# The maxima's score products take the step after: one offset in an attention kernel's interleaving

## The chip, the cores and the metric

The kernel runs on one core of one Trainium2 chip. The metric is the device time of one execution in microseconds (us), the median of several. The kernel before takes 2329.86 us (three runs, 2328.88 to 2336.1).

## The reference

The reference is a small network of several layers: an attention block with a feed-forward part, a routed layer of experts, a selective scan and a second gated layer. The change touches the attention alone. For two sequences of 2048 tokens and sixteen heads (eight of each of two attentions) of width 8 it computes:

```
q = (xin @ wq.T + bq).reshape(b, s, H, DK)
k = (xin @ wk.T + bk).reshape(b, s, H, DK)
v = (xin @ wv.T + bv).reshape(b, s, H, DK)
scores = jnp.einsum('bshd,bthd->bhst', q, k) * (1.0 / np.sqrt(DK))
a = jax.nn.softmax(scores, axis=-1)
o = jnp.einsum('bhst,bthd->bshd', a, v).reshape(b, s, DH)
```

## The kernel before, in words

The attention is cut into 32 units, one head of one sequence each. A unit's scores are computed twice. First the maximum of each row is needed: TensorE multiplies queries by keys, and VectorE reduces the product. This is done in 32 chunks a unit, each 128 queries by 1024 keys: two matmuls of 512 columns (L1593, the rows 0 to 47 and 64 to 111 of the tile `stacks`), into two banks of PSUM, and one reduction over 1024 values (L805). There are two such pairs of banks, so chunk c can be written only when the reduction of chunk c - 2 is done; that is the wait at the head of `max_scores`. When all 32 chunks are reduced, VectorE runs five small operations (L807 to L813) before it reduces the next unit's chunk 0. TensorE transposes their result (L1599), ScalarE copies it to `mT` (L1229), and SyncE's queue copies that twice into `stacks` (L518), from where the unit's exponentials take it as three more rows of the product.

Then the scores are computed again in 64 blocks of 128 keys by 512 queries (L1639), ScalarE takes the exponential into `probs` (L1241), and TensorE weighs the values with it (L1611). The blocks go in 44 steps a unit: one block in the even steps, in step 37 and in step 43, two blocks in the other odd steps. Steps take turns in two PSUM buffers, so the product of step e waits for the exponential of step e - 2. A weighing covers four blocks: eight matmuls in the trace, in two rounds of four, placed where its four exponentials lie at least two steps back: 16 a unit, at steps 1, 4, 7, 9, 12, 15, 17, 20, 23, 25, 28, 31, 33, 36, 39, 42. A half unit's sums stand in one bank, which ScalarE copies out (L1225) after the exponentials of steps 1 and 23, once the weighing of that step is done.

The order on TensorE is written out by hand. Each step issues, in this order: its one or two score products; the transpose, in step 37; one chunk of maxima, if the count by that step allows one; one weighing, if one is due. The maxima run ahead of the exponentials by a unit and ten chunks (`AHEAD`), so a unit's last chunk (31) and the next one's first (0) fall in the last third of a unit's steps. There are 32 chunks to 44 steps, so 12 steps have none. VectorE and ScalarE only follow: their order has no gaps to choose.

In this text a step's E is its score product, M the chunk of maxima, W the weighing.

Of the kernel before, what the change touches and what calls it, by code (L numbers as in the profile page):

```python
# [21 lines left out]
UNITS = G * B  # L22
# [10 lines left out]
STEPS = 2 * TCH  # L33
DFF = 512
CHUNKS = 2 * TCH
EXPS, TURN, AHEAD = 44, 37, 10
E, NG, KTOP, GTOP = 32, 8, 4, 4
CAP = int(1.25 * N * KTOP / E)
LN4, LN9 = NB, 5 * NB
# [73 lines left out]
def after(eng, sem, count):  # L113

    if not isinstance(count, int) or count > 0:
        eng.wait_ge(sem, count)
# [23 lines left out]
def build(nc, a, out):  # L140
# [3 lines left out]
    with ExitStack() as ctx:  # L144
# [1374 lines left out]
        def _(pe):  # L1519
# [77 lines left out]
            def turn_max(uu):  # L1597
                pe.wait_ge(spl_ready, uu + 1)
                pe.transpose(PT[:, 0:P], spl.rearrange("p l c -> p (l c)"), identb[:, :]).then_inc(mt_ready, 1)  # L1599

            def weigh(u, pair, w):

                pe.wait_ge(exp_done, EXPS * u + EXP_OF[4 * pair + 3] + 1)
                if pair % (TCH // 2) == 0:
                    after(pe, o_evac, 2 * u + pair // (TCH // 2))
                for odd in range(2):
                    kt = (2 * pair + odd) % TCH
                    for qb in range(2):
                        jg = 2 * odd + qb
                        at = (6 * (w % 2) + 4 * pair + jg) % RING * 512  # L1610
                        mm = pe.matmul(OB[32 * jg:32 * jg + 32, :], VH[w][:, kt, :], probs[:, at:at + 512],  # L1611
                                       start=(kt < 2), stop=(kt >= TCH - 2))
                mm.then_inc(pv_done, 1)

            def max_chunk(m):
                u, n = divmod(m, CHUNKS)
                if n == 0:
                    pe.wait_ge(qk_ld[u % 4], 192 * (u // 4 + 1))
                max_scores(u, n, u % 4)
# [8 lines left out]
            weighed, chunk = 0, CHUNKS + AHEAD  # L1628
            for u in range(UNITS):
                w, final = u % 4, u == UNITS - 1  # L1630
                pe.wait_ge(m_ld[w], 32 * (u // 4 + 1))
                for e, (first, blocks) in enumerate(EXP):
                    after(pe, exp_done, EXPS * u + e - 1)
                    if e == TURN + 2 and not final:
                        pe.wait_ge(mt_out, u + 2)
                    for i in range(blocks):
                        o = 64 * i
                        kt, q0 = (first + i) // 2 % TCH, (first + i) // 2 // TCH * 1024 + (first + i) % 2 * 512
                        mm = pe.matmul(EXB[e % 2][:, i, :], KS[w][o:o + KROWS + 3, kt * P:(kt + 1) * P], QS[w][o:o + KROWS + 3, q0:q0 + 512],  # L1639
                                       start=True, stop=True)  # L1640
                    mm.then_inc(sc_ready, 1)
                    if e == TURN and not final:
                        turn_max(u + 1)
                    if chunk < min(CHUNKS * UNITS, CHUNKS * (u + 1) + AHEAD + CHUNKS * (e + 1) // EXPS):
                        max_chunk(chunk)
                        chunk += 1
                    if e == 1:
                        pe.wait_ge(vh_ready, u + 1)
                    wu, pair = divmod(weighed, TCH)
                    if EXPS * wu + EXP_OF[4 * pair + 3] <= EXPS * u + e - 2:  # L1650
                        weigh(wu, pair, wu % 4)
                        weighed += 1
# [391 lines left out]
```

## Time and profile before

| | |
|---|---|
| median of three runs | 2329.86 us |
| the profiled execution | 2333.52 us |
| its span, first to last instruction | 2331.7 us |
| TensorE matmuls, busy | 1911.9 us, 82% |
| VectorE, busy | 1838.0 us, 79% |
| ScalarE, busy | 1425.0 us, 61% |

The span starts at the first instruction. The attention's steps lie between some 295 and 1640 us of it. Shares are of the whole span, so a stage has to be read from its own window.

### The profile page before, as it was taken

The page shows a single profiled execution, that of the slowest core. Times are in us where ns is not written, and L with a number is a line of the kernel's source. Part 1 is how long each engine was busy: PE and PEld are TensorE (multiplying, and loading weights), DVE is VectorE, ACT ScalarE, POOL GpSimd, SP SyncE. Part 2 cuts the span into 40 slices and gives each one's busy share as a digit, 9 for nine tenths or more (in the row PEclk, how much of TensorE's full clock was granted, in tenths as well). Part 3 has the DMA queues.
Part 4 walks back from the last instruction along what each step waited for, and adds up shares of the span by engine and source line. Part 5 has one row for each costly group of instructions (what it writes and reads, how often), then busy time and mean ns, then how long its engine had stood idle before and what let it go on. Part 6 is the DMA issues. An engine that isn't in the chain of part 4 may idle for free.

```text
span 2331.7 us, 33796 instructions
## 1 busy us (share of the span) xinstructions
PE 1911.9 (82%) x11886; PEld 727.7 (31%) x11886; DVE 1838.0 (79%) x2868; ACT 1425.0 (61%) x2159; POOL 298.3 (13%) x371
## 2 busy tenths in 40 slices
PE   2768488888888888888888888888898788679895
PEld 1324011221222112222222222221676444346563
DVE  3774789999999999999999999992334888658778
ACT  1113078787887878878878788778432334457542
POOL 0000100000000000422222222200003765000000
PEclk9976589999999999999999999999999878879896
DMA  4023101111111110211111111101575443222231
GB/s 123 19 74 122 54 22 52 32 51 39 34 55 33 40 50 31 73 39 36 45 33 45 37 34 45 47 9 30 161 205 157 119 128 87 77 83 58 74 94 37
DMA packets 156247, 150.76 MB, mean 65 GB/s; under 512 B 34490, under 2 KB 131774, under 8 KB 156094
## 3 DMA queue, kind: packets, MB, share of 16 engines
q1 hardware_dynamic: 147742, 131.48, 19.2%
q0 software_dynamic: 8352, 17.29, 2.6%
q8 instruction: 90, 1.47, 0.3%
q14 instruction: 63, 0.52, 0.1%
HBM read 85.81 MB, written 62.13 MB: 63 GB/s over the span
## 4 chain that ended last, share of the span: by engine, by line
PE 64%; DVE 14%; ACT 13%; issue 3%; DMA 2%; SPq 2%; POOL 0%; ACTq 0%; DVEq 0%; POOLq 0%
PE PS L1611 22%; PE PS L1639 14%; ACT probs L1241 10%; PE PS L1593 7%; DVE mxp L805 5%; PE PS L1686 3%; PE PS L1742 1%; PE PS L1842 1%; PE PS L1860 1%; PE PS L1673 1%; PE PS L1751 1%; ACT SG L1225 1%; PE PS L1863 1%; DMA xs_d<-SG 1%; PE PS L1845 1%
## 5 line engine op out<-in xcount | busy, mean ns | idle before, releaser
L805 DVE TENSOR_REDUCE mxp<-PS 128x1 f32<-128x1024 f32 x1024 | 1203.3, 1220 | 131.9 <-PE PS L1593 126.7
L1241 ACT ACTIVATE probs<-PS 128x512 f32<-128x512 f32 (+1 forms) x1408 | 1041.4, 790 | 261.9 <-PE PS L1639 259.4
L1639 PE MATMUL PS<-stacks 51*128 51x512 bf16 x2048 | 539.9, 385 | 139.3 <-ACT probs L1241 135.7
L1593 PE MATMUL PS<-stacks 48*128 48x512 bf16 x2048 | 513.6, 391 | 74.7 <-DVE mxp L805 51.2
L1611 PE MATMUL PS<-probs,VH 128*32 128x512 f32 x4096 | 547.3, 606 | 2.6 <-ACT probs L1241 0.7
L1639 PEld LDWEIGHTS PS<-stacks 51*128 51x128 bf16 x2048 | 136.0, 93 | 799.4 <-ACT probs L1241 761.5
L1510 POOL DMA_INDIRECT VP<-oe_d,ROWI x128 | 132.8, 1037 | 329.1 <-DMA oe_d<-stacks 266.5
L1492 POOL DMA_INDIRECT xe_d<-xn_s,rows_s x128 | 124.5, 973 | 382.9 <-PE PS L1611 353.6
L1593 PEld LDWEIGHTS PS<-stacks 48*128 48x128 bf16 x2048 | 121.5, 95 | 142.8 <-DVE mxp L805 96.1
L1611 PEld LDWEIGHTS PS<-probs,VH 128*32 128x32 f32 x4096 | 81.6, 108 | 191.4 <-issue 152.2
L826 DVE TENSOR_TENSOR stacks<-stacks,PS 128x640 f32<-128x640 f32 x32 | 26.2, 819 | 130.6 <-ACT stacks L1273 130.6
L1482 POOL COPY VH<-VP 128x128 f32<-128x128 f32 (+1 forms) x32 | 9.2, 293 | 744.6 <-PE PS L1611 599.4
L1686 PE MATMUL PS<-stacks,ews 128*128 128x320 f32 x256 | 76.4, 441 | 6.1 <-DVE stacks L826 4.3
L1742 PE MATMUL PS<-wa,wff 128*128 128x512 f32 x64 | 42.5, 821 | 25.7 <-ACT wa L1296 25.7
L1273 ACT ACTIVATE stacks<-PS 128x640 f32<-128x640 f32 x32 | 22.5, 704 | 59.9 <-PE PS L1686 59.9
L1686 PEld LDWEIGHTS PS<-stacks,ews 128*128 128x128 f32 x256 | 46.0, 189 | 27.5 <-issue 9.0
L1229 ACT ACTIVATE mT<-PS 48x128 bf16<-48x128 bf16 x32 | 8.2, 257 | 63.9 <-PE PS L1599 63.9
L1225 ACT ACTIVATE SG<-PS 128x512 f32<-128x512 f32 x64 | 38.2, 597 | 12.5 <-PE PS L1611 12.5
L1527 PE MATMUL PS<-ident,wa 128*128 128x128 f32 x32 | 8.9, 434 | 42.9 <-DVE wa L136 42.9
L1673 PEld LDWEIGHTS PS<-ews,stacks 128*128 128x128 f32 x320 | 40.7, 192 | 6.5 <-DVE stacks L826 1.6
L1673 PE MATMUL PS<-ews,stacks 128*128 128x128 f32 x320 | 41.0, 275 | 1.4 <-DVE stacks L832 1.4
L1842 PE MATMUL PS<-VP,cst 128*128 128x512 f32 x64 | 35.2, 677 | 7.0 <-DVE VP L1000 7.0
(351 smaller groups left out, 1997.9 us busy)
## 6 DMA issues: line engine op xcount, KB each, us to landing
xe_d<-zt SPq DMA_DIRECT2D x16, 640.0 KB
stacks<-xe_d SPq DMA_DIRECT2D x32, 320.0 KB, 3.6
oe_d<-stacks SPq DMA_DIRECT2D x32, 320.0 KB, 2.8
o_d<-SG SPq DMA_DIRECT2D x256, 32.0 KB, 1.6
ews<-in_ew_dram SPq DMA_DIRECT2D x33, 192.0 KB, 2.3
stacks<-ql_d SPq DMA_DIRECT2D x64, 96.0 KB
stacks<-kl_d SPq DMA_DIRECT2D x64, 96.0 KB
probs<-xs_d SPq DMA_DIRECT2D x18, 256.0 KB, 3.6
```

The source lines that it names most:

```text
L805: v.tensor_reduce(mxp[:, n // 2, n % 2:n % 2 + 1], MXB[n % 2].rearrange("p a c -> p (a c)"), X_AX, ALU.max).then_inc(mx_done, 1)
L1225: act.activation(OE[half][:, :], OB, ACT.Copy).then_inc(o_evac, 1)
L1241: act.activation(probs[:, at:at + n * 512], EXB[e % 2][:, 0:n, :].rearrange("p a c -> p (a c)"), ACT.Exp, scale=float(1.0 / np.sqrt(np.flo ...
L1492: pool.indirect_dma_start(xe_d, bass.IndirectOffsetOnAxis(rows_s[i][:, n:n + 1], 0), xn_s[i][:, :], None, bounds_check=E * CAP - 1, oob_is ...
L1510: pool.indirect_dma_start(GB[:, t % (2 * TB), n, :], None, oe_d, bass.IndirectOffsetOnAxis(ROWI[:, t, n:n + 1], 0), bounds_check=E * CAP, ...
L1593: mm = pe.matmul(MXB[n % 2][:, i, :], QS[w][o:o + MAXROWS, (n // 2) * P:(n // 2 + 1) * P], KS[w][o:o + MAXROWS, key:key + 512], start=True ...
L1611: mm = pe.matmul(OB[32 * jg:32 * jg + 32, :], VH[w][:, kt, :], probs[:, at:at + 512], start=(kt < 2), stop=(kt >= TCH - 2))
L1639: mm = pe.matmul(EXB[e % 2][:, i, :], KS[w][o:o + KROWS + 3, kt * P:(kt + 1) * P], QS[w][o:o + KROWS + 3, q0:q0 + 512], start=True, stop=True)
L1673: mm = pe.matmul(o, hhe[w % 2][:, t * P:(t + 1) * P], EW[w][:, 2, :], start=True, stop=True)
L1686: mm = pe.matmul(PS[:, 2 + 2 * m + h, 0:CAP // 2], EW[w][:, m, :], xeT[w % 2][:, h * CAP // 2:(h + 1) * CAP // 2], start=True, stop=True)
L1742: pe.matmul(PS[:, 2 + f % 2, :], wff1[:, f * P:(f + 1) * P], f_(wa[3]), start=True, stop=True).then_inc(f_ready, 1)
L1842: pe.matmul(PS[:, b, :], BELOW, scaled[:, b, :], start=True, stop=True)
```

## The change

In the count that allows a chunk of maxima, 12 is added before the division by 44 steps (`EARLY`).

```
-EXPS, TURN, AHEAD = 44, 37, 10
+EXPS, TURN, AHEAD, EARLY = 44, 37, 10, 12
...
-                    if chunk < min(CHUNKS * UNITS, CHUNKS * (u + 1) + AHEAD + CHUNKS * (e + 1) // EXPS):
+                    if chunk < min(CHUNKS * UNITS, CHUNKS * (u + 1) + AHEAD + (CHUNKS * (e + 1) + EARLY) // EXPS):
                         max_chunk(chunk)
                         chunk += 1
```

32 times 44 steps plus 12 still gives 32 chunks a unit. The steps without a chunk were 0, 3, 7, 11, 14, 18, 22, 25, 29, 33, 36, 40; they are now 1, 4, 8, 12, 15, 19, 23, 26, 30, 34, 37, 41. So the pattern stands one step later, with one chunk more already done at each of its places. Nothing changes on any engine but TensorE, and there no instruction of the attention is added or taken away.

TensorE in steps 10 to 15 of a unit (L1639 is E, L1593 is M, L1611 is W; neighbours of one line are joined). Before:

```order
L1639 MATMUL PS<-stacks 128x512
L1593 MATMUL PS<-stacks 128x512 x2
L1639 MATMUL PS<-stacks 128x512 x3
L1593 MATMUL PS<-stacks 128x512 x2
L1611 MATMUL PS<-probs,VH 32x512 x4
L1639 MATMUL PS<-stacks 128x512 x2
L1593 MATMUL PS<-stacks 128x512 x2
L1639 MATMUL PS<-stacks 128x512 x3
L1593 MATMUL PS<-stacks 128x512 x2
L1611 MATMUL PS<-probs,VH 32x512 x4
```

The same steps of TensorE now:

```order
L1639 MATMUL PS<-stacks 128x512
L1593 MATMUL PS<-stacks 128x512 x2
L1639 MATMUL PS<-stacks 128x512 x2
L1593 MATMUL PS<-stacks 128x512 x2
L1639 MATMUL PS<-stacks 128x512
L1611 MATMUL PS<-probs,VH 32x512 x4
L1639 MATMUL PS<-stacks 128x512 x2
L1593 MATMUL PS<-stacks 128x512 x2
L1639 MATMUL PS<-stacks 128x512
L1593 MATMUL PS<-stacks 128x512 x2
L1639 MATMUL PS<-stacks 128x512 x2
L1611 MATMUL PS<-probs,VH 32x512 x4
```

The chunks that stood between E and W in steps 12 and 15 now follow E of steps 11 and 14, which have no W.

TensorE in steps 29 to 33, around the chunks 31 and 0 of two units, before:

```order
L1639 MATMUL PS<-stacks 128x512 x3
L1593 MATMUL PS<-stacks 128x512 x2
L1639 MATMUL PS<-stacks 128x512 x2
L1593 MATMUL PS<-stacks 128x512 x2
L1611 MATMUL PS<-probs,VH 32x512 x4
L1639 MATMUL PS<-stacks 128x512
L1593 MATMUL PS<-stacks 128x512 x2
L1639 MATMUL PS<-stacks 128x512 x2
L1611 MATMUL PS<-probs,VH 32x512 x4
```

The same steps now:

```order
L1639 MATMUL PS<-stacks 128x512 x2
L1593 MATMUL PS<-stacks 128x512 x2
L1639 MATMUL PS<-stacks 128x512 x3
L1593 MATMUL PS<-stacks 128x512 x2
L1611 MATMUL PS<-probs,VH 32x512 x4
L1639 MATMUL PS<-stacks 128x512
L1593 MATMUL PS<-stacks 128x512 x2
L1639 MATMUL PS<-stacks 128x512 x2
L1593 MATMUL PS<-stacks 128x512 x2
L1611 MATMUL PS<-probs,VH 32x512 x4
```

Chunk 31 moved from step 30 to 29. Steps 31, 32 and 33 now have one chunk each, the last of them between E and W of step 33, where there was none.

TensorE in steps 37 to 39 (L1599 is the transpose), before:

```order
L1639 MATMUL PS<-stacks 128x512
L1599 MATMUL PS<-identb,spl 128x128
L1593 MATMUL PS<-stacks 128x512 x2
L1639 MATMUL PS<-stacks 128x512
L1593 MATMUL PS<-stacks 128x512 x2
L1639 MATMUL PS<-stacks 128x512 x2
L1593 MATMUL PS<-stacks 128x512 x2
L1611 MATMUL PS<-probs,VH 32x512 x4
```

The same steps now:

```order
L1639 MATMUL PS<-stacks 128x512
L1599 MATMUL PS<-identb,spl 128x128
L1639 MATMUL PS<-stacks 128x512
L1593 MATMUL PS<-stacks 128x512 x2
L1639 MATMUL PS<-stacks 128x512 x2
L1593 MATMUL PS<-stacks 128x512 x2
L1611 MATMUL PS<-probs,VH 32x512 x4
```

The chunk of step 37 went to step 36; steps 38 and 39 keep theirs, so there are two in a row ahead of this W and not three. Steps 26 to 28 changed in the same way.

## Rows read from the trace of the kernel before

**Rows 1.** The page's first part: busy us, share of the span, instructions.

```profile
PE 1911.9 (82%) x11886; PEld 727.7 (31%) x11886; DVE 1838.0 (79%) x2868; ACT 1425.0 (61%) x2159; POOL 298.3 (13%) x371
```

**Rows 2.** Busy time in the attention's steady stretch: PE, PEld, DVE, ACT, POOL, clock, DMA.

```profile
340.00:1592.00 1252.00, 1094.43 (x7642) 252.63 (x7641) 1143.16 (x1101) 1002.13 (x1398) 145.10 (x220) 1.00 0.13 41
```

**Rows 3.** The copies of a half unit's sums: duration ns, first and last start.

```profile
L1225 ACT ACTIVATE SG<-PS x57: 597/597/597, 405.0 to 1584.0; 128x512 f32<-128x512 f32 x57
```

**Rows 4.** Groups by line, 396 to 1592 us: busy us, mean ns | idle before.

```profile
L805 DVE TENSOR_REDUCE mxp<-PS 128x1 f32<-128x1024 f32 x908 | 1068.6, 1220 | 99.1 <-PE PS L1593 94.2
L1241 ACT ACTIVATE probs<-PS 128x1024 f32<-128x1024 f32 x569 | 581.9, 1023 | 94.2 <-PE PS L1639 92.4 <-issue 0.4
L1639 PE MATMUL PS<-stacks 51*128 51x512 bf16 x1819 | 479.3, 383 | 122.2 <-ACT probs L1241 119.7
L1593 PE MATMUL PS<-stacks 48*128 48x512 bf16 x1816 | 449.5, 380 | 27.2 <-DVE mxp L805 27.2
L1241 ACT ACTIVATE probs<-PS 128x512 f32<-128x512 f32 x681 | 403.5, 597 | 134.4 <-PE PS L1639 134.0
```

**Rows 5.** Chain that ended last, steps 1 to 15: start us, us, what.

```profile
803.82 0.22 PE PS L1593 x2
...
806.63 0.22 PE PS L1593 x2
806.85 0.99 PE PS L1611 x8
...
810.99 0.22 PE PS L1593 x2
...
814.04 0.22 PE PS L1593 x2
...
817.14 0.22 PE PS L1593 x2
```

**Rows 6.** Timeline of ScalarE: steps 1 and 23, the copies of sums.

```profile
805.10 0.60 ACT L1225 ACTIVATE SG<-PS 128x512 f32<-128x512 f32 x1 [0.16 <-PE PS L1611]
...
826.11 0.60 ACT L1225 ACTIVATE SG<-PS 128x512 f32<-128x512 f32 x1 [0.22 <-PE PS L1611]
```

**Rows 7.** Timeline of TensorE, steps 26 to 29: start us, us, what [idle before <-releaser].

```profile
827.85 0.39 PE L1639 MATMUL PS<-stacks 51*128 51x512 bf16 x1
...
828.92 0.39 PE L1639 MATMUL PS<-stacks 51*128 51x512 bf16 x1
829.78 0.39 PE L1593 MATMUL PS<-stacks 48*128 48x512 bf16 x2 [0.47 <-DVE mxp L805]
...
831.10 0.39 PE L1639 MATMUL PS<-stacks 51*128 51x512 bf16 x2
```

**Rows 8.** Timeline of VectorE around the end of a unit's maxima.

```profile
828.50 4.69 DVE L805 TENSOR_REDUCE mxp<-PS 128x1 f32<-128x1024 f32 x4 [0.65 <-PE PS L1593]
...
834.16 1.22 DVE L805 TENSOR_REDUCE mxp<-PS 128x1 f32<-128x1024 f32 x1
```

**Rows 9.** Timeline of steps 37 to 39: the transfer of `mT`, E and M.

```profile
839.62 1.62 SPq L518 DMA_DIRECT2D stacks<-mT  x2
...
839.66 0.39 PE L1639 MATMUL PS<-stacks 51*128 51x512 bf16 x2
840.54 0.39 PE L1593 MATMUL PS<-stacks 48*128 48x512 bf16 x2 [0.49 <-DVE mxp L805]
```

**Rows 10.** Timeline of TensorE: E of steps 31 and 32.

```profile
832.67 0.39 PE L1639 MATMUL PS<-stacks 51*128 51x512 bf16 x2 [0.75 <-ACT probs L1241]
...
834.20 0.39 PE L1639 MATMUL PS<-stacks 51*128 51x512 bf16 x1
```

**Rows 11.** DMA traffic of 836 to 848 us in 40 slices, GB/s.

```profile
GB/s 0 0 0 0 0 0 0 0 0 0 0 0 0 0 0 0 3 38 0 20 76 0 0 0 0 0 0 0 0 0 0 0 0 0 0 0 0 0 0 0
```

**Rows 12.** Timeline of TensorE: the next unit's first E.

```profile
844.91 0.38 PE L1639 MATMUL PS<-stacks 51*128 51x512 bf16 x1
```

## The prediction

> **What bounds the kernel now.** I first read the page's busy shares [rows 1]: TensorE leads, but over a whole span of different layers. So the second view is the window of the attention's steady stretch [rows 2]. There VectorE is busy 1143 of 1252 us (91%), TensorE 1094 (87%), ScalarE 1002 (80%), and TensorE's clock is granted in full (1.00, the 2.4 GHz level). No engine is full. The pace comes from the copies of half a unit's sums [rows 3]: 57 of them are 56 half units, so a unit takes (1584.0 - 405.0) / 28 = 42.1 us. The stretch of the next view, 1196 us, is 28.4 units.
>
> Third, the groups with the idle time before them [rows 4]. All three engines wait for one another: VectorE's reductions wait 99.1 us for TensorE, 3.5 us a unit; the exponentials wait 94.2 + 134.4 = 229 us for TensorE; TensorE waits 122 us for exponentials and 27.2 us for VectorE, the last being 0.96 us a unit. A ring of dependencies sets the pace, so what counts is what stands between one exponential and the next product. Fourth, the chain that ended last. It goes through every W, and an M is on it only where W follows at once, or where TensorE runs behind anyhow: in steps 1, 4, 8, 12 and 15 each shows as a piece of 0.22 us [rows 5], the two matmuls of a chunk side by side. Where an M is not on the chain (steps 2, 5, 6, 13 and others) TensorE is waiting for an exponential and the M fills the wait. So an M costs 0.22 us in two kinds of places and nothing elsewhere: in a W step, and in the step between two W that are two steps apart (8, 16, 24, 32). Fifth, the timeline where M itself waits. In step 28 E starts at 828.92 and M at 829.78, 0.86 us later where 0.22 is the rule: 0.64 us lost [rows 7]. In step 39 it is 840.54 - 839.66 - 0.22 = 0.66 us [rows 9]. Together 1.30 us a unit, more than the 0.96 that the groups book to the matmuls, since part is booked to the weight loads. Both times W stands behind the waiting M, and behind W the next E, and so ScalarE. Both are the third of three steps in a row with a chunk (26, 27, 28 and 37, 38, 39): two buffers, and a third chunk that must wait for the first one's reduction.
>
> **The change, part by part.** No instruction of the attention comes or goes, so there is no cost of work, only of place. Per unit:
>
> *Slots taken off the path.* Steps 4, 12 and 15 keep W and lose M, and step 8, between two W, loses its M: 4 x 0.22 = 0.88 us. Steps 1 and 23 lose theirs too, but behind their W ScalarE's copy waits, and it can start earlier only until it meets the exponential before it: it waited 0.16 and 0.22 us [rows 6], so 0.38 is gained. Sum 1.26. The M's go to steps 0, 3, 11, 14, 22, which have no W and lie beside exponentials; there TensorE's wait for the exponential hides them. Without that cover each would cost 0.22 again.
>
> *Slots put on the path.* Steps 7, 25, 33 and 36 have W, had no M and get one: 4 x 0.22 = 0.88. Net of both, 0.38 us less.
>
> *Waits that go.* The row of three 26, 27, 28 becomes 27, 28, 29, and 37, 38, 39 becomes 38, 39, 40: in steps 28 and 39 M is now the second, with a buffer free, and the third has no W behind it. That takes off the 1.30 us.
>
> *Waits that come.* Rows of three whose third step has W are now 5, 6, 7 and 31, 32, 33. From one E to its reduction is 828.50 - 827.85 = 0.65 us [rows 7, 8], a reduction takes 1.22, and the next M follows 829.78 - 829.72 = 0.06 after it. So M of step 7 can't start before 0.65 + 1.22 + 0.06 = 1.93 us after E of step 5. By itself it would come at 1.57 + 0.22 = 1.79: with a double exponential between them, E of a step follows E of two steps before by 832.67 - 831.10 = 1.57 [rows 7, 10]. Wait: 0.14. In step 33 the two units' boundary lies between. Four reductions from 828.50 take 4.69, so they are (4.69 - 1.22) / 3 = 1.16 apart and the fourth starts at 831.97; the next unit's first starts at 834.16, 2.19 later, for the five small operations [rows 8]. Counting from E of step 29, now with chunk 31: reduction 0.65, that of chunk 0 not before 2.84, done 4.06, M of step 33 from 4.12. TensorE would get there by 1.57 (to E of 31) + 1.53 (its E, M and W; 834.20 - 832.67 [rows 10]) + 0.44 (E and M of 32) + 0.22 (E of 33) = 3.76. Wait: 0.36. Together 0.50. Bounds: nothing, if the steps ahead run later than I count, and 1.30, the two waits of before. I take 0.5, since it comes from the rows of just these instructions. Before, step 33 had no chunk, and just that gap gave VectorE time.
>
> Sum per unit: -0.38 - 1.30 + 0.50 = -1.18 us. Units 0 to 30 see all of it, 31 x 1.18 = 36.6. The last unit has no maxima after step 30, so it keeps -1.26 and the 0.64 of step 28, and pays steps 7 (0.22 + 0.14) and 25 (0.22): -1.3. Together -38 us.
>
> *What else hangs on the place.* The transfer of the next unit's maxima begins after step 37 at 839.62 [rows 9] and its last traffic lies in the slice of 842.0 to 842.3 [rows 11]; the next unit's first E, which needs it, is at 844.91 [rows 12]. The steps between shrink by some 0.6 us, so over 1.5 us of slack stay. VectorE's idle 3.5 us a unit falls to some 2.4, still not full.
>
> The sum is made against the profiled execution: 2333.5 - 38 = 2295.5 us. That execution lies 3.7 us above the median of the runs shown, so the median should be 2329.9 - 38 = 2292 us.
>
> **The rivals.** *Only slots.* The waits move but don't shrink: new ones of 1.3 us for old ones of 1.3 us. For it: chunks and buffers are the same, and so is the share of work. Against it: the count of the third step above. Per unit -0.38; 31 x 0.38 is 12 us, and 0.8 of the last unit (1.26 less 0.44) makes it 13: 2317.
>
> *No new waits.* Steps 7 and 33 come late enough for their buffers. For it: 0.14 and 0.36 us are small beside sums of four or five rows. Per unit -1.68, or 54 us in all with the last unit: 2276.
>
> *VectorE is the bound.* It has the highest share [rows 2], its work is unchanged, and what an earlier M gains is given back as a later wait of TensorE for it: no change, 2330. Against it: of its 3.5 us of idle a unit nearly all is waiting for TensorE [rows 4]. The Trainium skill, in "Perfetto Trace Analysis", section "Identifying the Most-Contended Engine", says to take the engine with the highest occupancy as the bottleneck and work on that first, which would name VectorE here and expect nothing from TensorE's order alone; the trace agrees on the occupancy (91%) but shows the remaining idle time to be made by that order.
>
> *Slower: VectorE falls behind at the units' boundary.* The old waits don't go, since a backlog built up by three chunks right behind the five small operations is still there in steps 38 and 39, and steps 7 and 33 wait as long as 28 and 39 did. Per unit -0.38 + 1.30 = +0.92, 28 us in all: 2358. It decides from the point where the waits of a unit come to more than 1.68 us. Against it: steps 34 and 37 have no chunk, and after step 33 the next M's needed reduction ends ahead of it by my count.
>
> **How the numbers follow.** Forecast 0.64, only slots 0.15, no new waits 0.09, VectorE the bound 0.06, slower by the boundary 0.06. 0.3%, 7 us, is about what a measurement of this kernel can tell from no change. Faster by more: the first three less 0.02 for slots that come to less, 0.86; within: 0.08; slower: 0.06. The forecast's own range is 2282 to 2304 (a wait of 0.2 to 0.9 a unit in place of 0.5). The range for 8 in 10 takes in the two faster rivals, 2275 to 2320, and leaves out no change and slower.
>
> **What would show it.** In the profile after, the copies of sums should stand 40.9 us apart per unit (every second one). TensorE's waits for VectorE should be gone in steps 28 and 39 and be found in step 33 (0.36 us between the slots) and, short, in step 7. VectorE's idle before its reductions should fall by about a third. The chain that ended last should carry no M in steps 1, 4, 12, 15 and 23, and one in 7, 25, 33 and 36. The forecast is wrong if waits of 0.6 us or more stand in steps 7 or 33, if the interval is not shorter by 0.7 us or more, or if the time after the attention changes.

## The result, and the profile after

The changed kernel takes 2289.34 us (median of six runs, 2279.61 to 2293.11), the kernel before 2328.49 us in the runs beside it (2323.88 to 2336.1). The ratio is 0.9825, 95% interval 0.980 to 0.985: 39 us or 1.7% faster. The forecast was 2292 us.

The profiled execution spans 2289.1 us. The steady stretch of the attention, in the columns of [rows 2]:

```profile
340.00:1550.00 1210.00, 1094.22 (x7627) 251.76 (x7623) 1131.06 (x1098) 994.28 (x1394) 144.71 (x219) 1.00 0.13 42
```

The copies of half a unit's sums, against [rows 3]:

```profile
L1225 ACT ACTIVATE SG<-PS x57: 597/597/598, 399.2 to 1542.0; 128x512 f32<-128x512 f32 x57
```

A unit takes (1542.0 - 399.2) / 28 = 40.81 us, where it took 42.11: 1.29 us less. Read from each unit's first exponential to the next one's, the first unit is 1.95 us shorter, the next 29 are 1.29 each, the one after them 1.44, and the last unit not at all (37.39 us to its last exponential's end in both traces): 40.9 of the 42.6 us by which the two spans differ. The other 1.7 us lie ahead of the first exponential (at 295.5 us before, 293.8 now), where the change does nothing. The clock is granted in full in this stretch as before. The rest of the kernel didn't change: after the last exponential 692.5 us remain, as they did before.

The groups of the stretch 396 to 1550 us (28.3 units), against [rows 4]:

```profile
L805 DVE TENSOR_REDUCE mxp<-PS 128x1 f32<-128x1024 f32 x904 | 1055.8, 1219 | 69.5 <-PE PS L1593 67.0
L1241 ACT ACTIVATE probs<-PS 128x1024 f32<-128x1024 f32 x566 | 578.9, 1023 | 65.9 <-PE PS L1639 61.6 <-issue 0.2
L1639 PE MATMUL PS<-stacks 51*128 51x512 bf16 x1812 | 476.6, 384 | 104.2 <-ACT probs L1241 95.7 <-ACT mT L1229 6.5
L1593 PE MATMUL PS<-stacks 48*128 48x512 bf16 x1806 | 443.4, 381 | 6.4 <-DVE mxp L805 5.5
L1241 ACT ACTIVATE probs<-PS 128x512 f32<-128x512 f32 x678 | 401.3, 596 | 140.0 <-PE PS L1639 139.9
```

No operation is faster. The idle time before the reductions fell from 3.5 to 2.5 us a unit, the wait of the maxima's matmuls for VectorE from 0.96 to 0.19 (5.5 / 28.3).

In steps 28 and 39 M stood 0.86 and 0.88 us behind E [rows 7, 9]. The timeline of TensorE after (start us, us, what [idle before <-releaser]); the first two rows are E and W of step 28, the others those of step 39:

```profile
810.27 0.39 PE L1639 MATMUL PS<-stacks 51*128 51x512 bf16 x1 [0.25 <-ACT probs L1241]
...
810.80 1.07 PE L1611 MATMUL PS<-probs,VH 128*32 128x512 f32 x8
...
821.17 0.39 PE L1639 MATMUL PS<-stacks 51*128 51x512 bf16 x2 [0.23 <-ACT mT L1229]
...
821.71 1.06 PE L1611 MATMUL PS<-probs,VH 128*32 128x512 f32 x8
```

From E to W is now 0.53 and 0.54 us; the waits are gone. New ones stand in steps 7 and 33 (E, M, W of each):

```profile
790.99 0.39 PE L1639 MATMUL PS<-stacks 51*128 51x512 bf16 x2 [0.47 <-ACT probs L1241]
791.42 0.39 PE L1593 MATMUL PS<-stacks 48*128 48x512 bf16 x2
791.74 1.06 PE L1611 MATMUL PS<-probs,VH 128*32 128x512 f32 x8
...
815.14 0.59 PE L1639 MATMUL PS<-stacks 51*128 51x512 bf16 x2
815.92 0.39 PE L1593 MATMUL PS<-stacks 48*128 48x512 bf16 x2 [0.19 <-DVE mxp L805]
816.24 1.07 PE L1611 MATMUL PS<-probs,VH 128*32 128x512 f32 x8
```

Both M are released by VectorE; in step 7 it is the row of M's weight load that shows it:

```profile
791.41 0.10 PEld L1593 LDWEIGHTS PS<-stacks 48*128 48x128 bf16 x2 [0.33 <-DVE mxp L805]
```

A difference of the starts of E and M (0.78 us in step 33) over-reads the second wait. My reading is that a matmul queued behind another is recorded some 0.2 us before it runs: E of step 33, which follows M of step 32 at once, has 0.59 us on record for 0.39. So E to W (0.75 and 1.10 us) is the safer measure. What it is without a wait is shown below.

The copies of sums in ScalarE's timeline, the first with the exponentials ahead of it, against [rows 6]:

```profile
784.93 2.17 ACT L1241 ACTIVATE probs<-PS 128x512 f32<-128x512 f32 x3 [0.59 <-PE PS L1639]
787.03 0.60 ACT L1225 ACTIVATE SG<-PS 128x512 f32<-128x512 f32 x1
...
807.36 0.60 ACT L1225 ACTIVATE SG<-PS 128x512 f32<-128x512 f32 x1
```

They wait for nothing now; each starts as the exponential before it ends.

The chain that ended last, steps 24 to 33 (start us, us, what):

```profile
807.88 5.81 DVE mxp L805 x5
...
813.71 0.20 DVE nmx L807
...
814.73 1.14 DVE mxp L805
815.88 0.05 issue
815.92 0.39 PE PS L1593 x2
816.31 0.99 PE PS L1611 x8
```

Here is what I had not foreseen. From 807.88 to 815.88 the chain stays on VectorE: five reductions, the five small operations, one more reduction, without a gap, for a fifth of each unit; on the chain from 396 to 1550 us L805 went from 5.9% to 16.9%. These shares don't say what VectorE costs there. With a reduction of half the length (below) steps 24 to 32 keep their times to 0.01 us and only step 33 falls, by 0.37. Over this stretch VectorE's row and the ring of the other two engines are nearly equally long, and VectorE's is longer by 0.37 us.

Since every unit repeats to 0.01 us, a step can be read by itself: the median time from the start of its exponential to the next, over units 2 to 29, in us.

| step | before | after | |
|---|---|---|---|
| 1, 4, 12, 15, 23 | 1.67, 1.23, 1.25, 1.59, 1.73 | 1.45, 1.01, 1.03, 1.37, 1.51 | M gone from a W step: 0.22 each |
| 9 | 1.42 | 1.19 | M gone from step 8, between two W |
| 28, 39 | 1.89, 2.19 | 1.28, 1.53 | the wait gone |
| 7 | 1.37 | 1.79 | M and a wait |
| 33 | 1.20 | 1.78 | M and a wait |
| 25, 36 | 1.19, 0.97 | 1.29, 1.21 | M |

### The profile page after: what moved, and what is told of

The parts are those of the page before. It is cut to its first block, busy times and chain, and to the rows that moved or that the text cites. A ratio compares the mean times of both kernels' runs of the same rounds, so it can differ in the third digit from the quotient of the medians.

```text
span 2289.1 us, 33796 instructions
## 1 busy us (share of the span) xinstructions
PE 1912.8 (84%) x11886; PEld 728.1 (32%) x11886; DVE 1829.0 (80%) x2868; ACT 1420.3 (62%) x2159; POOL 298.6 (13%) x371
## 4 chain that ended last, share of the span: by engine, by line
PE 58%; DVE 21%; ACT 12%; issue 3%; DMA 2%; SPq 2%; POOL 0%; ACTq 0%; DVEq 0%; POOLq 0%
PE PS L1611 18%; PE PS L1639 13%; DVE mxp L805 11%; ACT probs L1241 8%; PE PS L1593 5%; PE PS L1686 3%; PE PS L1742 2%; PE PS L1842 1%; PE PS L1860 1%; PE PS L1673 1%; PE PS L1751 1%; ACT SG L1225 1%; PE PS L1863 1%; DMA xs_d<-SG 1%; PE PS L1845 1%
## 5 line engine op out<-in xcount | busy, mean ns | idle before, releaser
L805 DVE TENSOR_REDUCE mxp<-PS 128x1 f32<-128x1024 f32 x1024 | 1194.4, 1218 | 99.5 <-PE PS L1593 96.8
L1639 PE MATMUL PS<-stacks 51*128 51x512 bf16 x2048 | 538.7, 385 | 121.0 <-ACT probs L1241 110.8
L1593 PE MATMUL PS<-stacks 48*128 48x512 bf16 x2048 | 508.7, 392 | 52.5 <-DVE mxp L805 28.1
L1611 PE MATMUL PS<-probs,VH 128*32 128x512 f32 x4096 | 546.5, 606 | 1.0 <-ACT probs L1241 0.7
L1639 PEld LDWEIGHTS PS<-stacks 51*128 51x128 bf16 x2048 | 135.9, 93 | 769.3 <-ACT probs L1241 723.0
L1593 PEld LDWEIGHTS PS<-stacks 48*128 48x128 bf16 x2048 | 116.5, 95 | 154.1 <-DVE mxp L805 106.8
L1611 PEld LDWEIGHTS PS<-probs,VH 128*32 128x32 f32 x4096 | 81.0, 108 | 169.6 <-issue 138.9
L1273 ACT ACTIVATE stacks<-PS 128x640 f32<-128x640 f32 x32 | 22.5, 704 | 59.6 <-PE PS L1686 59.6
L1264 ACT ACTIVATE stacks<-PS 128x640 f32<-128x640 f32 x32 | 22.5, 703 | 29.3 <-PE PS L1665 29.3
```

The costliest lines, as they stand in the source:

```text
L805: v.tensor_reduce(mxp[:, n // 2, n % 2:n % 2 + 1], MXB[n % 2].rearrange("p a c -> p (a c)"), X_AX, ALU.max).then_inc(mx_done, 1)
L1593: mm = pe.matmul(MXB[n % 2][:, i, :], QS[w][o:o + MAXROWS, (n // 2) * P:(n // 2 + 1) * P], KS[w][o:o + MAXROWS, key:key + 512], start=True ...
```

## The experiments

These ran on three other chips, here A, B and C, where the kernel before takes 2421.6, 2434.0 and 2420.1 us. The changed one ran again on C and takes 2384.0. Its unit is the same there to 0.01 us (40.82, below), so the time of a unit, read in each trace from the copies of sums ahead of 900 us, and the ratio to the kernel before on the same chip are what is compared. The kernel before was not profiled on A, B or C: its 42.11 us a unit are the first chip's. The times in the expectations were meant for the first chip; their differences stand. In the traces of A, B and C two or three units from the middle on are disturbed, and the layers after the attention take 770 to 791 us for 692.5. In the changed kernel on C it is 773.6, on nearly the same busy time (the last exponential's end to the last instruction; the first row is the changed kernel on C, the second on the first chip; after the two times PE, PEld, DVE, ACT, POOL, clock, DMA):

```profile
1606.40:2380.00 773.60, 583.62 (x3214) 382.29 (x3214) 472.42 (x1437) 303.39 (x565) 134.10 (x130) 0.85 0.34 96
```

```profile
1596.60:2289.10 692.50, 572.39 (x3214) 379.05 (x3214) 472.06 (x1437) 302.87 (x564) 135.79 (x130) 0.89 0.38 108
```

On C 11.7% of this stretch's chain, some 90 us, stand in waits whose releaser is "another core or an unknown queue"; the 200 longest pieces of the first chip's chain have none. What these waits are stays open; no comparison of units rests on them.

| kernel | chip | a unit, us | ratio to before [95%] |
|---|---|---|---|
| before | the first | 42.11 | |
| changed | C | 40.82 | 0.9864 [0.984, 0.989] |
| first half | A | 41.22 | 0.9894 [0.985, 0.994] |
| second half | A | 41.70 | 0.9962 [0.994, 0.999] |
| before, short reduction | A | 41.03 | 0.9803 [0.976, 0.985] |
| changed, short reduction | A | 40.25 | 0.9707 [0.967, 0.975] |
| AHEAD 11 | B | 42.11 | 1.0016 [1.000, 1.004] |
| EARLY 24 | B | 42.38 | 1.0044 [1.002, 1.007] |
| changed, gap at 33 | B | 40.87 | 0.9858 [0.982, 0.990] |
| changed, unit's end later | C | 40.59 | 0.9848 [0.982, 0.988] |
| gaps chosen, first | B and C | 40.03 | 0.9731 and 0.9763 |
| gaps chosen, second | C | 39.88 | 0.9745 [0.971, 0.978] |

**Half of the move each.** The steps without a chunk are listed and counted; only the list differs.

```
-EXPS, TURN, AHEAD = 44, 37, 10
+EXPS, TURN, AHEAD = 44, 37, 10
+WITHOUT = (1, 4, 8, 12, 15, 19, 23, 25, 29, 33, 36, 40)
...
-                    if chunk < min(CHUNKS * UNITS, CHUNKS * (u + 1) + AHEAD + CHUNKS * (e + 1) // EXPS):
+                    if chunk < min(CHUNKS * UNITS, CHUNKS * (u + 1) + AHEAD + sum(i not in WITHOUT for i in range(e + 1))):
```

> The first half of the move alone: the steps without a chunk are 1, 4, 8, 12, 15, 19, 23 as in the changed kernel, and 25, 29, 33, 36, 40 as before. Theory A (a chunk costs its 0.22 us where a weighing follows, and the wait for a buffer in some steps): steps 1, 4, 8, 12, 15, 23 give back 0.22 us each, 1.3 us, and step 7 costs 0.4; 0.9 us a unit less than before's 42.1, 28 us in all, about 2300 us. The waits in steps 28 and 39 stay as they were. Theory B (VectorE's pace alone decides, and only its waits in steps 28 and 39 were worth something): no change, 2328 us.

The second has `WITHOUT = (0, 3, 7, 11, 14, 18, 22, 26, 30, 34, 37, 41)`.

> The second half alone: the steps without a chunk are 0, 3, 7, 11, 14, 18, 22 as before, and 26, 30, 34, 37, 41 as in the changed kernel. Theory A: steps 28 and 39 give back 0.60 + 0.66 us, steps 25, 33 and 36 cost 0.09 + 0.58 + 0.24; 0.35 us a unit less, 11 us in all, about 2317 us, and with the first half it adds up to the whole. Theory B: the whole gain of 39 us, 2289 us.

The copies of sums (25 of them, 12 units) of the first half and of the second:

```profile
L1226 ACT ACTIVATE SG<-PS x25: 597/597/598, 382.0 to 876.6; 128x512 f32<-128x512 f32 x25
```

```profile
L1226 ACT ACTIVATE SG<-PS x25: 597/597/598, 377.6 to 878.1; 128x512 f32<-128x512 f32 x25
```

494.6 / 12 = 41.22 and 500.5 / 12 = 41.71 us: 0.89 and 0.40 us less than before, 0.9 and 0.35 expected. They add up to 1.29, the whole. Theory B falls: more than two thirds of the gain came without touching the waits of steps 28 and 39.

**A reduction of half the values.** VectorE reduces the first 512 of a chunk's 1024 values and leaves the other half out.

```
-v.tensor_reduce(mxp[:, n // 2, n % 2:n % 2 + 1], MXB[n % 2].rearrange("p a c -> p (a c)"), X_AX, ALU.max)
+v.tensor_reduce(mxp[:, n // 2, n % 2:n % 2 + 1], MXB[n % 2][:, 0, :], X_AX, ALU.max)
```

> The kernel before with every reduction of a chunk over 512 of its 1024 values only (the maximum is then that of half the keys); all matmuls stay, and VectorE takes about half the time. Theory A: only the waits in steps 28 and 39 go, 1.26 us a unit, 39 us: 2289 us. Theory B (VectorE is the bound): far more, VectorE's whole lead over the others, some 3 us a unit or 90 us: 2240 us.

> The changed kernel with the same short reduction. Theory A: only the waits in steps 7 and 33 go, 0.2 + 0.36 = 0.56 us a unit, 17 us: 2272 us; between this and the kernel before with the short reduction there are then only slots, 0.4 to 0.5 us a unit or 12 to 17 us. Theory B: the two with the short reduction are the same. A third reading (C), that what helps is that each place in the steps has one chunk more behind it: the difference between the two stays at 39 us.

The copies of sums, 27 or 13 units, of the kernel before with the short reduction and of the changed one:

```profile
L1225 ACT ACTIVATE SG<-PS x27: 597/597/597, 346.6 to 880.0; 128x512 f32<-128x512 f32 x27
```

```profile
L1225 ACT ACTIVATE SG<-PS x27: 597/597/598, 361.0 to 884.2; 128x512 f32<-128x512 f32 x27
```

The timeline of TensorE in the first, E and W of its step 28:

```profile
800.77 0.39 PE L1639 MATMUL PS<-stacks 51*128 51x512 bf16 x1
...
801.41 1.06 PE L1611 MATMUL PS<-probs,VH 128*32 128x512 f32 x8
```

And in the second, E and W of step 7, then of step 33 with M between:

```profile
767.41 0.39 PE L1639 MATMUL PS<-stacks 51*128 51x512 bf16 x2 [0.47 <-ACT probs L1241]
...
767.95 1.07 PE L1611 MATMUL PS<-probs,VH 128*32 128x512 f32 x8
...
791.36 0.59 PE L1639 MATMUL PS<-stacks 51*128 51x512 bf16 x2
791.58 0.59 PE L1593 MATMUL PS<-stacks 48*128 48x512 bf16 x2
792.09 1.07 PE L1611 MATMUL PS<-probs,VH 128*32 128x512 f32 x8
```

(880.0 - 346.6) / 13 = 41.03 and (884.2 - 361.0) / 13 = 40.25 us a unit. Though VectorE's main work was nearly halved (a reduction takes 0.69 us for 1.22), the kernel before gains only 1.07 us a unit: 0.53 in step 28 and 0.54 in step 39, and no other step moves by over 0.01. A wait of some 0.1 stays in each (E to W of step 28 is 0.64 us, for 0.53 without one), so the 1.26 expected was right but for this rest. The changed kernel gains 0.57: E to W of step 33 falls from 1.10 to 0.73 and of step 7 from 0.75 to 0.54, so its waits cost 0.37 + 0.21. Between the two with the short reduction 0.79 us remain. Less the two rests of 0.1 that is some 0.6 us of slots; I had expected 0.4 to 0.5, reading C 1.29 and theory B none.

The whole kernel gains more than its units: 46 us by the medians on A (2421.6 to 2375.8), where 31 units explain 33. About as much as the rest lies ahead of the first exponential, where the first 42 chunks are made: from the first reduction to there it is 33.1 us with the short reduction, for 47.5 in the kernel before. VectorE's work on the partial maxima in that stretch of the kernel before (window, us, DVE busy):

```profile
248.00:295.50 47.50, 46.71 (x43) 0.50 0.16 58
```

Busy for 46.7 of 47.5 us, VectorE is the bound in that stretch, though not in the units.

**The lead alone.** `AHEAD` 11 for 10 in the kernel before.

> The kernel before with the maxima one chunk further ahead (AHEAD 11 for 10): the steps without a chunk are those of before, each place has one chunk more behind it. Theory A: nothing in the pattern changes, only the units' boundary moves from steps 30 and 31 to 28 and 30, behind the wait of step 28: within 3 us of before, 2328 us. Reading C (the lead is what helps): the gain of 39 us, 2289 us.

42.11 us a unit, ratio 1.0016 with 1 in the interval: a chunk more of lead is worth nothing. Reading C falls; it is the places.

**One more step later.** `EARLY` 24 for 12.

> The changed kernel with EARLY 24 for 12, the pattern one more step later: no chunk in steps 2, 5, 9, 13, 16, 20, 24, 27, 31, 35, 38, 42. Theory A by counting: chunks in 12 steps with a weighing and in 2 between weighings two apart, 14 against before's 16 (0.44 us less); rows of three that end at a weighing in steps 1, 12 and 23, waits of some 0.7 + 0.64 + 0.14 = 1.5 us against 1.26. About 0.2 us a unit less than before, 6 us: 2322 us, so nearly all of the gain of EARLY 12 is gone. Theory C (later is better): faster than the changed kernel, under 2285 us.

42.38 us, 0.27 more than before, where I had counted 0.2 less: the slower side, ratio 1.0044. The waits in steps 1, 12 and 23 came as counted (0.64, 0.64 and 0.15 by the steps' intervals). Missed was step 33. There E, M and W are

```profile
837.34 0.59 PE L1639 MATMUL PS<-stacks 51*128 51x512 bf16 x2
838.35 0.39 PE L1593 MATMUL PS<-stacks 48*128 48x512 bf16 x2 [0.41 <-DVE mxp L805]
838.66 1.07 PE L1611 MATMUL PS<-probs,VH 128*32 128x512 f32 x8
```

E to W 1.32 us, for 0.73 without a wait: 0.59 us. No row of three chunks ends there (step 31 has none). This M is chunk 2 and waits for the reduction of chunk 0, which starts behind the five small operations, at 837.07 us in VectorE's timeline; they do what the third chunk does elsewhere. The count "three in a row ahead of a W" was too simple.

**The gap put back to 33.** `WITHOUT = (1, 4, 8, 12, 15, 19, 23, 26, 30, 33, 37, 41)`.

> The changed kernel with the gap of step 34 put back to 33, so that no chunk stands before the weighing right after the units' boundary. Theory A by plain addition: 0.58 us a unit come back in step 33, and steps 34, 35, 36 become a row of three that ends at a weighing, which costs 0.14 to 0.6: between 0 and 0.4 us a unit less, 2276 to 2289 us. If a wait of VectorE can't be moved away but only along, exactly nothing: 2289 us.

40.87 us, 0.06 more than the changed kernel. Step 33 gave back its 0.58 as expected, and step 36, now third of a row of three, took 0.61 (E, M, W):

```profile
817.06 0.39 PE L1640 MATMUL PS<-stacks 51*128 51x512 bf16 x1
817.92 0.39 PE L1594 MATMUL PS<-stacks 48*128 48x512 bf16 x2 [0.47 <-DVE mxp L806]
818.24 1.07 PE L1612 MATMUL PS<-probs,VH 128*32 128x512 f32 x8
```

E to W is 1.18, as in step 28 before. The wait moved along, as the second reading had it.

**The end of a unit later.** In the changed kernel, VectorE's five small operations go behind the next unit's chunk 2, with two buffers of partial maxima.

```
+                    if n == 2 and uu > 0:
+                        unit_end(uu - 1)
```

> The changed kernel with VectorE's five small operations at the end of a unit's maxima moved behind the next unit's chunk 2 (two buffers of partial maxima in turn); TensorE's order is the changed kernel's but for one transpose at the start. Theory A: the wait in step 33 comes from these five operations between two reductions, so step 33 falls by 0.37 us, from 1.78 to 1.41; some of it may come back in steps 36 or 39, where the chunk now has the operations ahead of it. 0.15 to 0.37 us a unit, 5 to 11 us less than the changed kernel on the same chip. Rival: the wait in 33 is two buffers and three chunks in a row, as in 28 and 39 before; then step 33 keeps its 1.78.

40.59 us, 0.22 less. Step 33 falls from 1.78 to 1.41, and 0.15 comes back in step 39. E and W of its step 33, 0.74 us apart:

```profile
810.71 0.59 PE L1644 MATMUL PS<-stacks 51*128 51x512 bf16 x2
...
811.45 1.06 PE L1616 MATMUL PS<-probs,VH 128*32 128x512 f32 x8
```

That is the value without a wait, so the wait of step 33 came from these operations. (In the second half of this run a unit takes 40.70.) In time it is 3 us by the medians beside the changed kernel, 2381.0 and 2384.0, which the intervals don't tell apart.

**Gaps chosen by the reasons found.** `WITHOUT` as in the expectations.

> The gaps chosen by the reasons found: no chunk in steps 1, 7, 10, 15, 18, 23, 26, 31, 32, 36, 39, 42. Chunks stand in 8 steps with a weighing and 3 between, 11 against before's 16 and the changed kernel's 14, and one row of three ends at a weighing (step 4, some 0.6 us). Theory A: before's 42.1 less 5 x 0.22 and less 1.26 - 0.6, 40.3 us a unit, or 39.9 if step 4 waits less: 2260 to 2275 us. Theory B (VectorE near its bound): no better than the changed kernel, 2289 us.

> Another choice by the same reasons: no chunk in steps 1, 4, 8, 12, 20, 23, 26, 31, 32, 36, 39, 42. Chunks stand in 7 steps with a weighing and 2 between, 9 slots on the path against 11 of the choice with gaps at 1, 7, 10, 15, 18, and the wait in step 4 (0.44) is exchanged for that in step 7 (0.20). Plain addition: 0.68 us a unit less than that choice's 40.03, 39.35. But seven chunks in a row (13 to 19) ask for more than VectorE gives there, so waits of up to 0.7 come in steps 15 to 19: between 39.4 and 40.1 us a unit, so 0 to 20 us less on the same chip. If VectorE is near its bound by now, exactly nothing.

> The changed kernel, to have it on the chip of the others: every unit 40.8 us as before, and about 0.98 of the kernel before on this chip.

> The choice with gaps in steps 1, 7, 10, 15, 18, 23, 26, 31, 32, 36, 39, 42 once more, beside the changed kernel on one chip: 40.03 us a unit, 31 x 0.78 = 24 us less than the changed kernel.

The changed kernel on C, then the second choice, 27 copies or 13 units each:

```profile
L1225 ACT ACTIVATE SG<-PS x27: 597/597/598, 354.0 to 884.6; 128x512 f32<-128x512 f32 x27
```

```profile
L1226 ACT ACTIVATE SG<-PS x27: 597/597/598, 373.1 to 891.5; 128x512 f32<-128x512 f32 x27
```

40.82 and 39.88 us; the first choice, read in the same way, 40.03, between the 39.9 and 40.3 expected, with a wait of 0.44 us in step 4. Beside one another on C the changed kernel, the second choice and the first took 2384.0, 2356.1 and 2363.7 us. Both choices beat both kernels; the second's interval of the ratio, 0.971 to 0.978, lies clear of the changed kernel's 0.984 to 0.989. By addition it should have been 39.35; 0.5 us went to steps 15, 17 and 20 (0.14, 0.30 and 0.09 by their intervals), in and just behind a row of seven chunks. In step 17 M stands 0.71 us behind E, W 1.03, for 0.73 in steps without a wait.

```profile
785.19 0.59 PE L1640 MATMUL PS<-stacks 51*128 51x512 bf16 x2
785.90 0.39 PE L1594 MATMUL PS<-stacks 48*128 48x512 bf16 x2
786.22 1.07 PE L1612 MATMUL PS<-probs,VH 128*32 128x512 f32 x8
```

## Why the prediction was right

*Slots off the path*, forecast 1.26 us a unit: 5 x 0.22 + 0.23 = 1.33. Right in kind. Steps 1 and 23 gave the full 0.22; I had taken the idle time shown before the copies, 0.16 in step 1, as all that could be had. But where ScalarE doesn't wait, the copy starts before the exponential ahead of it has ended (787.03, and 784.93 + 2.17 = 787.10), so there was 0.07 us more room than the idle time shows.

*Slots on the path*, forecast 0.88: about 0.22 in step 7, 0.21 in 33 and 0.24 in 36, but 0.10 in step 25, together 0.77. The mis-sized term is step 25. Its W goes to the bank that the copy of step 23 frees, and in the trace before that copy ends at 826.71 and W starts at 826.85. E to W is 0.64 us there before, 0.73 now. My reading is that part of the added M filled that wait. I had not counted it, and no run here takes the copy away, so this is argued only.

*Waits that go*, forecast 1.30: steps 28 and 39 fell by 0.61 and 0.66, 1.27. The short reduction shows that they were waits for VectorE.

*Waits that come*, forecast 0.50 (0.14 and 0.36): 0.21 and 0.37, by the short reduction. That of step 33 is due to the five operations at the unit's end, as forecast, which the run with them moved shows.

Sum: -1.33 + 0.77 - 1.27 + 0.58 = -1.25, and smaller shifts in steps 17 to 42 make it -1.29, for -1.18 forecast.

*The last unit*, forecast -1.3: wrong. The prediction says that it has no maxima after step 30. But the maxima run a unit and ten chunks ahead, so the unit that stops at step 30 is the one before the last, and the last has none; it takes 37.39 us in both traces. The one before it gained 1.44 and the first 1.95, for 1.18 each. So the units gained 40.9 us for the 38 forecast, and that this term was wrong hardly shows in the total. *VectorE's idle time* a unit should have fallen to 3.5 - 1.18 = 2.3 by the prediction's own numbers, not 2.4; it fell to 2.5.

*What else hangs on the place*: from the transfer of `mT` to the next unit's first E it was 5.29 us [rows 9, 12]. Now, in the timeline of SyncE and TensorE:

```profile
821.12 1.62 SPq L518 DMA_DIRECT2D stacks<-mT  x2
```

```profile
825.76 0.38 PE L1639 MATMUL PS<-stacks 51*128 51x512 bf16 x1
```

4.64 us, 0.65 less, where 0.6 was forecast, and E shows no wait.

*The rivals.* "Only slots" is a part of the truth: slots were some 0.6 of the 1.29. "VectorE is the bound" is wrong for the units of the kernel before, as the short reduction and the first half show; in the changed one it costs 0.58 us a unit, in steps 7 and 33. The rule of the Trainium skill ("Perfetto Trace Analysis", "Identifying the Most-Contended Engine") pointed to VectorE by its 91%. With its reductions nearly halved the kernel before gained 1.07 us of a 42.11 us unit, and an order on another engine, which takes away no work, 1.29. In the whole kernel the short reduction gained more, 46 us (on A) for 36 (on C), by the stretch ahead of the first unit. So the highest occupancy did name an engine worth work, but not what its units waited for. That the rule would expect nothing from TensorE's order was my own addition; the section doesn't say so. "Slower at the boundary" did not come here, but its mechanism is real: one step later still (`EARLY` 24) the new waits outweigh the rest and the kernel is slower than before.

The signs named beforehand came: 40.8 us a unit for 40.9, idle before the reductions down by about a third (3.5 to 2.5), waits in steps 33 and 7 and none in 28 and 39. One failed: the chain need not carry an M in step 25, since it is on VectorE there.

## What to carry to other kernels

Where an order is written out by hand and several engines wait in a ring, price each place, not each instruction: the same chunk cost 0.22 us ahead of a long matmul group, nothing beside an exponential, and, on top, up to 0.66 us of waiting as the third in a row on two buffers. Such prices add up well (0.89 + 0.40 = 1.29) until the other engine runs without gaps over some stretch; there a wait taken out of one step can come back in a later one. Look for that engine's small extra work at a boundary before a regular pattern is laid over it.

## What the runs showed of the hardware

By my reading a matmul that is queued behind another is recorded before it runs. In step 33 M starts 0.22 us after E in the records where nothing waits, yet W comes 0.73 us after E, for 0.54 in step 7, whose E is not queued (0.59 and 0.39 us on record). So the wait of step 33, read from M's start, was 0.56 us, and taking it away gave 0.37. E to W gave the right value in both steps.

A chain can run on one engine for 8 us without a gap and that engine still cost only 0.37 us there: the chain shows which row ended last, not by how much.

The changed kernel's units take the same time on the first chip and on C, to 0.01 us (40.81 and 40.82), while the layers after them differ by 81 us.
